# Value copies and both layer normalisations on ScalarE, and the value bias added once per batch

## The chip, the cores and the metric

The kernel runs on one core of a Trainium2 chip. A core has five engines with instruction streams of their own: TensorE (PE, with PEld for its weight loads), VectorE (DVE), ScalarE (ACT), GpSimd (POOL) and SyncE (SP, which issues loads). They meet only through semaphores. The metric is the time in microseconds (us) that the device needs for one execution, as a median of several.

## The reference

The input x is 8 sequences of 2048 rows of 256 numbers. Two blocks follow each other, each with a residual and a layer normalisation without weights:

```python
q, k, v = _heads(x, Wq, bq), _heads(x, Wk, bk), _heads(x, Wv, bv)      # 16 heads of 16
qp = relu(einsum('bhsd,hdf->bhsf', q, rw)) + EPS                       # 64 features a head
kp = relu(einsum('bhsd,hdf->bhsf', k, rw)) + EPS
kv = einsum('bhsf,bhsd->bhfd', kp, v)
out = einsum('bhsf,bhfd->bhsd', qp, kv) / (einsum('bhsf,bhf->bhs', qp, kp.sum(axis=2)) + EPS)
x = layernorm(x + out @ Wo + bo)
# feed-forward: a gated MLP of width 1024 plus a mixture over 1024 experts
mlp = silu(x @ Wg + bg) * (x @ Wu + bu) @ Wd + bd
w = silu(x . down_embed[idx]) * softmax(scores); experts = sum_k w * up_embed[idx]   # top 8 of 1024, 4 heads
x = layernorm(x + mlp + experts)
```

Since v = x Wv + bv, the product kv equals (kp times x Wv) plus bv times the sum of kp over the sequence; the kernel has this sum anyway, as a 33rd column of ones beside the values.

## The kernel before, in words

Rows are handled in 32 groups of 512 (four tiles of 128 rows), four groups to a batch (a sequence). The loop has 35 iterations, numbered 4 to 38. In iteration `it` five stages work on different groups: key work of group it (`kv`: transposes, k, v, key features `kp`, and `sum`, which adds kp times v into `kv_sum`), attention of group it-4 (`at`), routing of group it-5 (`rt`), the feed-forward of group it-6 (`ff`) and the last normalisation and the store of group it-7 (`last`). The first four groups' key work is done in a fill ahead of the loop. Iterations 7 to 31 have all five stages; I call them the full ones. From 32 on there is no key work.

An iteration has 8 steps, c = 0 to 7. Each step does 128 columns of the feed-forward: on TensorE the products gate, up and dots into two PSUM banks in turn (`ring`), then the output products into `y_bank`. ScalarE applies Silu to gate and to dots (`ff_gate`, `ff_dots`), VectorE forms `gate` and `wexp` from them (`ff_h`, `ff_wexp`). Between these stand small pieces of the other stages, which share four PSUM banks (`step_bank`) in a fixed rotation: a piece can start only when the bank's last user has been read. Every engine's order is written out by hand in its own `body`, so nothing is reordered: an instruction that waits holds up all behind it on its engine.

What the change touches:
- `v` (L914): VectorE adds the bias bv to two tiles of values (128x512) on their way from PSUM to `v_sb`, at steps 2 and 5.
- `norm_scale` (L404 to L409): GpSimd turns variances into 1/sqrt by two small instructions, add and power.
- `norm1` (L982): VectorE normalises the attention output `x1`, four instructions of 128x256, at step 7, behind the last `sum`. TensorE's transposes `next` (L517) of x1 wait for it.
- `norm2` (L1074): the same for the output rows `y_sb`, at step 0 behind `wexp`, before `choose(0)`, whose first instruction writes `cand` (L1004). GpSimd's store waits for it.
- routing: VectorE's `scores`, `choose`, `keep` (L1020), `add_head` (L1033, L1036); GpSimd's `spread` (L430) writes `grid`; ScalarE's Exp (L812, `rt_use`) stands between scores and choose. Exp and Silu need different tables, so a table load stands ahead of each.
- `highs` (ScalarE, L768) and `lows` (VectorE, L894): the rounded and the remaining part of q and k, needed by TensorE's feature products and before their bank is free.

The first two of these lines end step 0 on ScalarE with the Exp; the others begin step 1, with the Silu of gate and then the second half of q's highs:

```python
                    if rt and c == 0:
                        rt_use(0)
...
                    if ff:
                        ff_gate(c)
                    if at:
                        for use in AT_EARLY[c]:
                            at_use(*use)
```

## Time and profile before

| | |
|---|---|
| median of 3 executions | 3860.46 us (3854.98 to 3862.65) |
| profiled execution | 3858.18 us, its span 3856.4 us |
| TensorE busy | 3674.8 us (95%) |
| VectorE busy | 3076.9 us (80%) |
| ScalarE busy | 1339.8 us (35%) |
| GpSimd busy | 1675.2 us (43%) |
| mean granted TensorE clock | 0.978 |

The span is the time from the first to the last instruction of the profiled execution. Busy shares are averages: TensorE is busy nearly all the time, VectorE four fifths of it, ScalarE a third. In the timeline, entries of one line that follow each other are merged (x4 is four instructions). A matmul's start is that of its place in TensorE's queue, so a group behind another can begin some tenths of a microsecond before its first column moves.

### The profile page before, as it was taken

The numbers are of one execution on the slowest core, as the hardware profiler recorded it, in microseconds if no ns is written. First come the engines' busy times: TensorE is split into PE (matmuls) and PEld (weight loads), VectorE is DVE, ScalarE is ACT, GpSimd is POOL, SyncE is SP. The second block draws the span as 40 slices with busy tenths as digits, with TensorE's granted clock in tenths as the row PEclk, the third lists the DMA queues.
The fourth block names the chain that finished last, engine by engine and source line by source line (L and its number), as shares of the span: only waits on it lengthen the run. The fifth ranks groups of instructions, "written<-read, shape, count | busy, mean of one in ns | idle before, by whom it ended". The sixth has DMA issues, their size and how long they took to land. (4 is left out here: it accounts for less than half of the span.)

```text
span 3856.4 us, 51959 instructions
## 1 busy us (share of the span) xinstructions
PE 3674.8 (95%) x19388; PEld 3095.6 (80%) x19388; DVE 3076.9 (80%) x5947; ACT 1339.8 (35%) x1990; POOL 1675.2 (43%) x1004
## 2 busy tenths in 40 slices
PE   8969999999999999999999999999999999999988
PEld 7758888888788888888888887888888888777766
DVE  2388888888788878888878888888888888999983
ACT  3323333333333333333333333333333333333321
POOL 0144444444444444454444454444444444555541
PEclk8769999999999999999999999999999999999999
DMA  3000000000000000000000000000000000000000
GB/s 111 17 12 6 12 17 17 17 12 12 12 18 17 17 12 12 15 14 17 17 12 12 17 12 17 17 12 12 17 12 17 17 6 12 12 11 12 6 6 12
DMA packets 23337, 61.15 MB, mean 16 GB/s; under 512 B 5552, under 2 KB 10032, under 8 KB 23088
## 3 DMA queue, kind: packets, MB, share of 16 engines
q1 hardware_dynamic: 18480, 41.04, 3.4%
q0 software_dynamic: 4608, 16.78, 1.1%
q8 instruction: 157, 2.57, 0.3%
q14 instruction: 92, 0.75, 0.1%
HBM read 41.04 MB, written 16.78 MB: 15 GB/s over the span
## 5 line engine op out<-in xcount | busy, mean ns | idle before, releaser
L430 POOL TENSOR_TENSOR grid<-ex 128x1024 f32<-128x1024 f32 x512 | 1245.6, 2440 | 626.3 <-ACT ex L812 286.7
L1020 DVE SCALAR_TENSOR_TENSOR grid<-grid,best 128x1024 f32<-128x1024 f32 x512 | 736.8, 1439 | 31.0 <-POOL grid L430 30.2
L1036 DVE SCALAR_TENSOR_TENSOR prob<-grid,rz,prob 128x1024 f32<-128x1024 f32 x384 | 694.6, 1809 | 3.4
L687 PE MATMUL y_bank<-wd_sb,gate 128*128 128x256 f32 x2048 | 625.2, 387 | 15.6 <-DVE wexp L1058 15.6
L689 PE MATMUL y_bank<-up_sb,wexp 128*128 128x256 f32 x2048 | 612.3, 381 | 0.0
L595 PE MATMUL ring<-x1T_hl,downT_hl 128*128 128x512 f32 x1536 | 417.5, 407 | 19.0 <-ACT gate L817 19.0
L689 PEld LDWEIGHTS y_bank<-up_sb,wexp 128*128 128x128 f32 x2048 | 391.7, 191 | 54.0
L595 PE MATMUL ring<-x1T_hl,wg_hl 128*128 128x512 f32 x1536 | 423.6, 411 | 7.9 <-DVE gate L1052 7.7
L595 PE MATMUL ring<-x1T_hl,wu_hl 128*128 128x512 f32 x1536 | 418.0, 407 | 0.0
L421 POOL TENSOR_SCALAR qp<-qp 128x512 f32<-128x512 f32 x256 | 217.0, 848 | 432.4 <-ACT qp L803 421.0
L687 PEld LDWEIGHTS y_bank<-wd_sb,gate 128*128 128x128 f32 x2048 | 355.9, 192 | 58.3 <-issue 29.9
L595 PEld LDWEIGHTS ring<-x1T_hl,downT_hl 128*128 128x128 f32 x1536 | 277.5, 189 | 85.7 <-ACT gate L817 30.4
L822 ACT ACTIVATE wexp<-ring 128x512 f32<-128x512 f32 x256 | 153.1, 598 | 556.2 <-PE ring L595 555.5
L595 PEld LDWEIGHTS ring<-x1T_hl,wu_hl 128*128 128x128 f32 x1536 | 284.5, 188 | 71.8 <-issue 14.4
L817 ACT ACTIVATE gate<-ring,bg_sb 128x512 f32<-128x512 f32 x256 | 176.4, 689 | 474.2 <-PE ring L595 473.2
L595 PEld LDWEIGHTS ring<-x1T_hl,wg_hl 128*128 128x128 f32 x1536 | 276.0, 189 | 75.4 <-issue 14.9
L783 ACT ACTIVATE kp<-step_bank 128x512 f32<-128x512 f32 x236 | 140.8, 597 | 410.7 <-PE step_bank L559 410.1
L416 POOL TENSOR_TENSOR xb<-xb,bo_sb 128x1024 f32<-128x1024 f32 x32 | 75.2, 2350 | 470.6 <-PE step_bank L517 470.6
L407 POOL TENSOR_SCALAR rstd<-mv 128x4 f32<-128x4 f32 x64 | 15.0, 234 | 570.5 <-DVE mv L945 570.5
L621 PEld LDWEIGHTS step_bank<-kv_blocks,qp 128*128 128x128 f32 x2048 | 252.2, 195 | 8.7 <-DVE ex L996 1.6
L621 PE MATMUL step_bank<-kv_blocks,qp 128*128 128x34 f32 x2048 | 243.5, 275 | 1.3 <-DVE ex L996 1.3
L566 PEld LDWEIGHTS step_bank<-v_sb,kp 128*128 128x128 f32 x1856 | 231.3, 197 | 10.6 <-issue 3.5
(146 smaller groups left out, 5693.2 us busy)
## 6 DMA issues: line engine op xcount, KB each, us to landing
xb<-in_L_attn_x SPq DMA_DIRECT2D x34, 512.0 KB, 3.5
out_y<-x POOLq DMA_DIRECT2D x32, 512.0 KB, 3.1
xa<-in_L_attn_x SPq DMA_DIRECT2D x30, 512.0 KB, 3.4
prob<-in_L_ffn_down_embed SPq DMA_DIRECT2D x1, 1024.0 KB, 5.9
prob<-in_L_ffn_Wg SPq DMA_DIRECT2D x1, 1024.0 KB, 8.7
prob<-in_L_ffn_Wu SPq DMA_DIRECT2D x1, 1024.0 KB, 10.5
wd_sb<-in_L_ffn_Wd SPq DMA_DIRECT2D x1, 1024.0 KB, 11.4
up_sb<-in_L_ffn_up_embed SPq DMA_DIRECT2D x1, 1024.0 KB, 12.0
```

The costliest lines, as they stand in the source:

```text
L421: pool.tensor_scalar(qp[:, j % 4], qp[:, j % 4], ATTN_EPS, 1.0, ALU.add, ALU.mult).then_inc(qp_eps, 1)
L430: pool.tensor_tensor(grid[:, h % 2], bcast(ex[:, h, 0:NX].unsqueeze(2), [P, NX, NK]), bcast(ex[:, RH + h, 0:NK].unsqueeze(1), [P, NX, NK]) ...
L566: mm = pe.matmul(bank[:, c * VW:(c + 1) * VW], lane.kp[:, c * P:(c + 1) * P], lane.v[:, j % 2, c, :], start=(c == 0), stop=(j < T - 1), sk ...
L595: mm = pe.matmul(bank[:], st if swap else wt, wt if swap else st, start=(k == 0 and i == 0), stop=(k == KD - 1 and i == 2))
L621: mm = pe.matmul(at_bank[:, (2 * t + c) * W:(2 * t + c + 1) * W], qp[:, (2 * j + c) % 4, t * P:(t + 1) * P], kv_blocks[:, 2 * j + c].rearr ...
L687: pe.matmul(rows, gate[:, c % 2, t * P:(t + 1) * P], wd_sb[:, c, :], start=(c == 0 and t % 2 == 0), stop=False, skip_group_check=True)
L689: mm = pe.matmul(rows, wexp[:, c % 2, t * P:(t + 1) * P], up_sb[:, c, :], start=False, stop=(c == C - 1), skip_group_check=True)
L783: read_by(act.activation(lane.kp[:, (j % 2) * G:(j % 2 + 1) * G], bank[:], ACT.Relu), "kv", a, kind, j)
L817: act.activation(gate[:, c % 2], ring[c % 2][:], ACT.Silu, bias=bg_sb[:, c:c + 1]).then_inc(ring_act, 1)
L822: act.activation(wexp[:, c % 2], ring[c % 2][:], ACT.Silu).then_inc(ring_act, 1)
L1020: marks["keep", h] = rt_steps.mark(dve.scalar_tensor_tensor(out=g, in0=g, scalar=best[:, h, TOP - 1:TOP], in1=g, op0=ALU.is_ge, op1=ALU.mult))
L1036: ins = dve.scalar_tensor_tensor(out=row, in0=g, scalar=rz[:, h:h + 1], in1=row, op0=ALU.mult, op1=ALU.add, accum_out=mass[:, 0:1] if h == ...
```

## The change

ScalarE copies the values without a bias. Both normalisations become an Identity activation with a scale (rstd) and a bias per row, on ScalarE; GpSimd prepares the bias, minus mean times rstd, with two more small instructions. `norm1` now stands behind `ff_gate(7)` and ahead of the last key features' relu, `norm2` behind the Exp of step 0 and ahead of `ff_gate(1)`. At the end of each batch VectorE adds bv times the summed key features to `kv_sum` before it copies it to `kv_blocks`; clearing `kv_sum` is a memset now.

```diff
@@ GpSimd
                 pool.tensor_scalar(rstd[:], mv[:, :, 1], LN_EPS, None, ALU.add).then_inc(s_own, 1)
-                pool.wait_ge(s_own, g + 1)
-                pool.tensor_tensor(rstd[:], rstd[:], neg_half[:], ALU.pow).then_inc(s_out, 1)
+                pool.tensor_scalar(mv[:, :, 0], mv[:, :, 0], -1.0, 1.0, ALU.mult, ALU.mult).then_inc(s_own, 1)
+                pool.wait_ge(s_own, 3 * g + 1)
+                pool.tensor_tensor(rstd[:], rstd[:], neg_half[:], ALU.pow).then_inc(s_own, 1)
+                pool.wait_ge(s_own, 3 * g + 3)
+                pool.tensor_tensor(mv[:, :, 0], mv[:, :, 0], rstd[:], ALU.mult).then_inc(s_out, 1)
@@ ScalarE
-                if kind in ("v", "sum"):
+                if kind == "sum":
                     return
                 bank = bank_of("kv", a, kind, j)
                 act.wait_ge(*full("kv", a, kind, j))
-                if kind == "turn":
+                if kind == "v":
+                    read_by(act.copy(lane.v[:, :, :, 0:2 * DK],
+                                     bank[:].rearrange("p (t c w) -> p t c w", t=2, c=FC)), "kv", a, kind, j)
+                elif kind == "turn":
...
+                def norm1():
+                    act.wait_ge(rstd1_ready, m + 1)
+                    for t in range(T):
+                        act.activation(x1[:, t, :], x1[:, t, :], ACT.Identity, bias=mv1[:, t, 0:1],
+                                       scale=rstd1[:, t:t + 1]).then_inc(x1_ready, 1)
+
+                def norm2():
+                    act.wait_ge(rstd2_ready, it - LAST_LAG + 1)
+                    for t in range(T):
+                        act.activation(y_sb[:, t, :], y_sb[:, t, :], ACT.Identity, bias=mv2[:, t, 0:1],
+                                       scale=rstd2[:, t:t + 1]).then_inc(y_ready, 1)
+
...
                     if ff:
                         ff_gate(c)
+                    if at and c == C - 1:
+                        norm1()
                     if at:
                         for use in AT_EARLY[c]:
                             at_use(*use)
...
                     if rt and c == 0:
                         rt_use(0)
+                    if last and c == 0:
+                        norm2()
@@ VectorE
-                dve.tensor_scalar(kv_sum[:, :, 0:2 * DK], bv_sb[:].rearrange("p (c w) -> p c w", c=FC),
-                                  ATTN_EPS * S, None, ALU.mult).then_inc(sum_cleared, 1)
+                dve.memset(kv_sum[:, :, 0:2 * DK], 0.0).then_inc(sum_cleared, 1)
...
-                elif kind == "v":
-                    dve.wait_ge(*full("kv", a, kind, j))
-                    read_by(dve.tensor_tensor(lane.v[:, :, :, 0:2 * DK],
-                                              bank[:].rearrange("p (t c w) -> p t c w", t=2, c=FC),
-                                              bcast(bv_sb[:].rearrange("p (c w) -> p c w", c=FC).unsqueeze(1),
-                                                    [P, 2, FC, 2 * DK]), ALU.add), "kv", a, kind, j)
...
-                    if at and c == 7:
-                        norm1()
...
-                    if last and c == 0:
-                        norm2()
...
             def batch_end(b):
 
                 dve.wait_ge(*drained("kv", (b + 1) * BG - 1, "sum", T - 1))
+                bias = cand[:].rearrange("p h a b -> p (h a b)").rearrange("p (c w) -> p c w", c=FC)
+                dve.tensor_tensor(bias, bv_sb[:].rearrange("p (c w) -> p c w", c=FC),
+                                  bcast(kv_sum[:, :, 2 * DK:VW], [P, FC, 2 * DK]), ALU.mult).then_inc(sum_biased, 1)
+                dve.wait_ge(sum_biased, 2 * b + 1)
+                dve.tensor_tensor(kv_sum[:, :, 0:2 * DK], kv_sum[:, :, 0:2 * DK], bias, ALU.add).then_inc(sum_biased, 1)
+                dve.wait_ge(sum_biased, 2 * b + 2)
```

ScalarE from the Exp of step 0 (a table load and the activation that writes `ex`) to the highs of k at step 1 in a full iteration, after the change (line numbers are those of the changed file):

```order
L818 ACT_TABLE_LOAD [waits rt_dve]
L818 ACTIVATE ex<-ex 128x576 [waits bank_read1]
L829 ACTIVATE x<-x,mv,rstd 128x256 [waits rstd2_ready]
L829 ACTIVATE x<-x,mv,rstd 128x256 x3
L835 ACT_TABLE_LOAD [waits y_full]
L835 ACTIVATE gate<-ring,bg_sb 128x512 [waits ring_full]
L771 ACTIVATE qT_hl<-step_bank,bq_sb 64x512 [waits bank_full3]
L771 ACTIVATE qT_hl<-step_bank,bq_sb 64x512
```

Before, the same stretch had no normalisation between the Exp and the table load for Silu:

```order
L812 ACT_TABLE_LOAD [waits rt_dve]
L812 ACTIVATE ex<-ex 128x576 [waits bank_read1]
L817 ACT_TABLE_LOAD [waits y_full]
L817 ACTIVATE gate<-ring,bg_sb 128x512 [waits ring_full]
L768 ACTIVATE qT_hl<-step_bank,bq_sb 64x512 [waits bank_full3]
L768 ACTIVATE qT_hl<-step_bank,bq_sb 64x512
```

The four instructions of `norm2` (they write x, which y_sb shares with x1) now stand ahead of the Silu of gate and of the second half of q's highs. On VectorE the same place before, from the first lows of q to the first add of a head:

```order
L894 SCALAR_TENSOR_TENSOR qT_hl<-step_bank,bq_sb,qT_hl 64x512 [waits q_high] x2
L1077 TENSOR_SCALAR x<-x,mv,rstd 128x256 [waits rstd2_ready]
L1077 TENSOR_SCALAR x<-x,mv,rstd 128x256 x3
L1004 TENSOR_TENSOR cand<-ex 128x256 [waits rt_exp]
L1009 MAX best<-cand 128x8 [waits rt_dve,pool_prep]
L1009 MAX best<-cand 128x8 x3
L1012 TENSOR_REDUCE zsum<-best 128x4 [waits rt_dve]
L1014 RECIPROCAL rz<-zsum 128x4 [waits rt_dve]
L1020 SCALAR_TENSOR_TENSOR grid<-grid,best 128x1024 [waits spread_ready]
L894 SCALAR_TENSOR_TENSOR qT_hl<-step_bank,bq_sb,qT_hl 64x512 [waits q_high] x2
L1033 TENSOR_SCALAR prob<-grid,rz 128x1024 [waits bank_full0,rt_dve]
```

After the change the two L1077 rows are gone and all others stand as they were: VectorE goes from the lows of q straight to `cand`, which waits for the Exp. And VectorE at the start of an iteration that opens a batch, after the change (`x<-y_bank` is the first read of the output rows):

```order
L1056 TENSOR_TENSOR prob<-prob,mass 128x1 [waits rt_dve]
L1140 TENSOR_TENSOR cand<-bv_sb,kv_sum 128x256 [waits bank_read1]
L1143 TENSOR_TENSOR kv_sum<-kv_sum,cand 128x8x32 [waits sum_biased]
L1147 COPY kv_blocks<-kv_sum 64x8x16 [waits sum_biased]
L1148 COPY kv_blocks<-kv_sum 64x8
L1147 COPY kv_blocks<-kv_sum 64x8x16
L1148 COPY kv_blocks<-kv_sum 64x8
L880 MEMSET kv_sum 128x8 [waits blocks_ready]
L881 MEMSET kv_sum 128x8x32
L1078 TENSOR_TENSOR x<-y_bank,bd_sb 128x512 [waits y_stored,bank_full3,y_full]
```

The two L114x instructions are new here, each waited for by the next; the last memset took the place of a 128x256 multiply.

## Rows read from the trace of the kernel before

**Rows 1.** Busy time by stretch, full iterations: length, engines (instructions), TensorE clock, DMA

```profile
420.00:3300.00 2880.00, 2804.98 (x15093) 2373.70 (x15092) 2372.98 (x4641) 1041.22 (x1542) 1294.33 (x775) 1.00 0.04 14
```

**Rows 2.** Waits of PE from 420 to 3300 us: total, times, longest

```profile
PE step_bank L517 <- DVE ex L996: 36.0, 24, 2.2
...
PE step_bank L531 <- DVE kT_hl L894: 35.3, 25, 1.4
```

**Rows 3.** Timeline, one full iteration: start, duration, work [idle before <- releaser]

```profile
2018.13 1.38 DVE L1077 TENSOR_SCALAR x<-x,mv,rstd 128x256 f32<-128x256 f32 x4
...
2018.58 0.69 ACT L812 ACTIVATE ex<-ex 128x576 f32<-128x576 f32 x1
...
2019.43 0.42 DVE L1004 TENSOR_TENSOR cand<-ex 128x256 f32<-128x256 f32 x1
...
2020.58 0.69 ACT L817 ACTIVATE gate<-ring,bg_sb 128x512 f32<-128x512 f32 x1
...
2021.16 1.38 ACT L768 ACTIVATE qT_hl<-step_bank,bq_sb 64x512 fp32r<-64x512 f32 x2
2021.44 1.93 PE L595 MATMUL ring<-x1T_hl,downT_hl 128*128 128x512 f32 x6
...
2022.96 1.51 DVE L894 SCALAR_TENSOR_TENSOR qT_hl<-step_bank,bq_sb,qT_hl 64x512 fp32r<-64x512 f32 x2
...
2024.51 1.01 DVE L1033 TENSOR_SCALAR prob<-grid,rz 128x1024 f32<-128x1024 f32 x1
...
2036.00 1.99 PE L531 MATMUL step_bank<-wv_sb,xaT 128*128 128x256 f32 x8 [1.42 <-DVE kT_hl L894]
```

**Rows 4.** Groups of instructions by line: busy us, mean ns | idle before, releaser

```profile
L783 ACT ACTIVATE kp<-step_bank 128x512 f32<-128x512 f32 x236 | 140.8, 597 | 410.7 <-PE step_bank L559 410.1
...
L963 DVE TENSOR_TENSOR x<-step_bank,den 128x256 f32<-128x256 f32 x128 | 54.3, 424 | 4.4
```

**Rows 5.** Timeline of ScalarE, preparation: a copy of 256 columns

```profile
81.92 0.43 ACT L756 COPY grid<-ring 128x256 f32<-128x256 f32 x1
```

**Rows 6.** Timeline, an iteration without key work, about the same place

```profile
3493.23 1.66 PE L595 MATMUL ring<-x1T_hl,downT_hl 128*128 128x512 f32 x6 [0.99 <-ACT gate L817]
...
3498.05 0.75 DVE L1033 TENSOR_SCALAR prob<-grid,rz 128x1024 f32<-128x1024 f32 x1
```

**Rows 7.** Timeline, end of the full iteration of Rows 3

```profile
2104.35 0.69 ACT L817 ACTIVATE gate<-ring,bg_sb 128x512 f32<-128x512 f32 x1
...
2109.94 1.87 PE L566 MATMUL step_bank<-v_sb,kp 128*128 128x33 f32 x16
```

**Rows 8.** Timeline, start of an iteration that opens a batch

```profile
976.35 1.07 PE L517 MATMUL step_bank<-ident_r,xa 128*128 128x128 f32 x4 [2.21 <-DVE ex L996]
```

**Rows 9.** Timeline of SyncE, residual loads of three successive iterations

```profile
829.34 0.33 SPq L375 DMA_DIRECT2D xb<-in_L_attn_x  x1
...
944.14 0.33 SPq L375 DMA_DIRECT2D xb<-in_L_attn_x  x1
...
1061.59 0.33 SPq L375 DMA_DIRECT2D xb<-in_L_attn_x  x1
```

**Rows 10.** Busy time by stretch, right behind the wait of Rows 8

```profile
978.00:982.00 4.00, 4.00 (x11) 2.23 (x10) 0.82 (x2) 1.65 (x5) 0.00 (x0) 0.77 0.42 131
```

**Rows 11.** Timeline, end of the first iteration

```profile
169.44 1.04 POOL L409 TENSOR_TENSOR rstd<-rstd,neg_half 128x4 f32<-128x4 f32 x1
169.78 2.58 PE L566 MATMUL step_bank<-v_sb,kp 128*128 128x33 f32 x16 [0.79 <-ACT kp L783]
...
176.13 1.94 PE L517 MATMUL step_bank<-ident_r,x 128*128 128x128 f32 x8 [1.90 <-DVE x L985]
```

**Rows 12.** Timeline, end of the second iteration

```profile
257.36 1.94 PE L566 MATMUL step_bank<-v_sb,kp 128*128 128x33 f32 x16 [0.79 <-ACT kp L783]
...
258.39 1.07 POOL L409 TENSOR_TENSOR rstd<-rstd,neg_half 128x4 f32<-128x4 f32 x1
...
274.98 1.94 PE L517 MATMUL step_bank<-ident_r,x 128*128 128x128 f32 x8 [14.28 <-DVE x L985]
```

More of the change, by code:

```diff
@@ L147, in block_kernel @@
         k_high, xs_ready = sem("k_high"), sem("xs_ready")
-        blocks_ready, sum_cleared = sem("blocks_ready"), sem("sum_cleared")
+        blocks_ready, sum_cleared, sum_biased = sem("blocks_ready"), sem("sum_cleared"), sem("sum_biased")
         xa2_loaded = sem("xa2_loaded")
@@ L906, in kv_use @@
                 lane, i = in_lane(a)
-                if kind not in ("k", "v", "sum"):
+                if kind not in ("k", "sum"):
                     return
@@ L980, in norm1_stats @@
                     statistics(x1, stats, mv1, at_steps)
-                def norm1():
-                    dve.wait_ge(rstd1_ready, m + 1)
-                    for t in range(T):
-                        dve.tensor_scalar(x1[:, t, :], x1[:, t, :], mv1[:, t, 0:1], rstd1[:, t:t + 1],
-                                          ALU.subtract, ALU.mult).then_inc(x1_ready, 1)
                 def scores(t):
@@ L1072, in y_rows @@
                     statistics(y_sb, stats, mv2, y_steps)
-                def norm2():
-                    dve.wait_ge(rstd2_ready, f + 1)
-                    for t in range(T):
-                        dve.tensor_scalar(y_sb[:, t, :], y_sb[:, t, :], mv2[:, t, 0:1], rstd2[:, t:t + 1],
-                                          ALU.subtract, ALU.mult).then_inc(y_ready, 1)
                 def uses(kinds):
```

## The prediction

> **What bounds the kernel now.** I read the busy time by stretch first. In the 25 full iterations (420 to 3300 us) TensorE is busy 2805 of 2880 us, so an iteration lasts 115.2 us and TensorE idles 3.0 us of it; VectorE is busy 2373, ScalarE 1041 [rows 1]. Nothing can be won there beyond 75 us, and an engine that makes TensorE wait loses at once. Then the table of waits, for what those 75 us are: 36.0 us at the second transpose of xa at step 0, whose bank `scores(0)` on VectorE must read first, and 35.3 us (25 times, never over 1.4) at the values of step 2, whose bank the second `lows` of k must free [rows 2]. Both name VectorE as the late engine. Last the timeline between them, to see what VectorE hangs on, since taking work off it pays only where it has no other wait.
>
> There the reader sees this. `norm2` runs on VectorE at 2018.13 for 1.38 us, beside the Exp, which ends at 2019.27; `cand` starts at 2019.43, as soon as either allows [rows 3]. ScalarE then switches tables, and the Silu of gate(1) ends at 2021.27. TensorE's dots(1) begins at 2021.44 in the same PSUM bank that this Silu reads, so it has 0.12 us to spare if it starts 0.05 us behind the Silu, as it did in an iteration where it had to wait (the Silu ended at 3493.18, dots at 3493.23 [rows 6]). Then come q's second highs at 2021.16, and VectorE's lows of them at 2022.96. So the tightest place of the iteration is on ScalarE, the engine that is idle two thirds of the time, right where the change puts `norm2`.
>
> **The change, part by part.**
>
> *norm2 in the full iterations.* The trace has no Identity of 128x256 with two per-row operands. A copy of 256 columns took 0.43 us [rows 5]. One per-row bias cost 0.09 (Silu with bias 0.69 [rows 3], Relu without 0.597 [rows 4], both 128x512). Neighbours overlap by 0.11: the Silu starts at 2020.58 and runs 0.69, the highs start at 2021.16 [rows 3]. So one takes 0.43 + 2 x 0.09 = 0.61, and starts 0.50 after the last; four need 0.1 + 4 x 0.50 = 2.1 us. This I take. Bounds: four of 0.43 with that overlap and free operands, 1.4; four of 0.69 without overlap, 2.8. The rule against the change is in the Trainium skill, ScalarE: Activation LUTs, Rules for kernel authors: multiply and add belong on VectorE. The trace agrees as far as it goes, 1.38 us for the four on VectorE [rows 3] against my 2.1. By the same page's figures (What ACT_TABLE_LOAD costs: 186 ns, 0.833 ns a column, 93 ns for each per-row operand, 93 ns of overlap) the four would be 2.07 us, an estimate that would leave the sum as it is.
>
> rstd was there before 2018.13, when VectorE used it [rows 3]; even 1.1 us later it is in time for an Exp that ends at 2019.27. So everything on ScalarE from the Silu of gate(1) on moves by T = 2.1. Two engines feel it.
> TensorE: dots(1) starts at 2021.27 + 2.1 + 0.05 = 2023.42 and not at 2021.44. About 0.3 of the difference is only queue time (a group behind a long one is stamped early: this one shows 1.93 us, one that had waited 1.66 [rows 3, 6]). TensorE is late by 1.7.
> VectorE: the lows could start 0.72 us behind the highs, at 2021.88 + 2.1 = 2023.98, and not at 2022.96: 1.0 late. The scaling that follows took 1.01 beside a GpSimd `spread` [rows 3] and takes 0.75 alone [rows 6]; moved later it runs alone, so 0.26 comes back, and VectorE is 0.75 late. From there to the lows of k it has no idle time in the timeline, so it keeps these 0.75.
> Both meet at the values of step 2 (2036.00, wait 1.42 [rows 3]). TensorE arrives 1.7 late, which its wait takes in but for 0.3; VectorE frees the bank 0.75 late. The later one decides: **0.75 us an iteration**, and 25 x 0.75 = **19 us**. With T between 1.4 and 2.8 this is 0.05 to 1.45 an iteration, 1 to 36 us.
> VectorE's 1.38 us less at step 0 is worth 0.1 at most, since `cand` waits for the Exp.
>
> *norm1 and the values, full iterations: nothing.* The Silu of gate(7) ends at 2105.04, norm1 then runs to 2107.2 and the last relu of kp to 2107.8; the `sum` on TensorE that needs it starts at 2109.94 [rows 7]. What VectorE saves lies ahead of its wait for the x1 transposes, whose place TensorE's full queue sets. If that cover were gone, norm1 would cost up to 2.1 each time. The value copies (some 0.6 us) fall into idle time of ScalarE: it waits 410 us in all for the kp products alone [rows 4]. On VectorE they stood ahead of waits for an Exp or for TensorE.
>
> *Batch starts.* At six of the eight (iterations 8 to 28) VectorE's copies to kv_blocks lie on the way to scores(0), and TensorE's wait is 2.21 [rows 8] where it is 1.25 otherwise (36.0 us in 24 waits, six of them of 2.21, leave 18 of 1.26 [rows 2]): their 0.96 us goes straight into the time. Added are two 128x256 operations like the one of 0.424 us [rows 4], each waited for, 0.95 in all; the memset may save 0.1. 6 x 0.85 = **5 us**, with 3 and 7 as ends.
>
> *The clock.* Two of those six waits of 2.21 us were followed by a lowered clock, 1.2 instead of 2.4 GHz for part of a stretch (mean 0.77 [rows 10]). The iteration around it, from one residual load to the next, took 117.45 us; the one before took 114.80 [rows 9]. Less the 0.96 that is 1.7 us for one fall. The waits become 3.1 us; I count two more falls, **3 us** (0 to 7).
>
> *The first two iterations.* In iteration 4 norm1 stands ahead of the last relu of kp and waits for GpSimd. Its power ends at 170.48; with two more small instructions (0.3 each, a guess between nothing and the power's own 1.04) rstd is there at 171.1, norm1 ends at 173.2, the relu at 173.8, and `sum` starts 4.1 us after its 169.78 [rows 11]. It and what belongs to it took until 174.2; the transposes come at 178.3 and not at 176.13: +2.2. In iteration 5 TensorE waited 14.28 us for norm1, which VectorE reached only behind its routing [rows 12]. On ScalarE it ends at about 262.2, `sum` starts at 262.9, the transposes at 266.5 and not 274.98. Of those 8.5 us VectorE's routing gives back half (the lows of x1 and the clamp still stand behind it, it is earlier by norm1's 1.4 and does not wait again for x1): -4.7. It also drops two value additions in iterations where it is the late engine, -0.9. Together **-3 us** (-7 to +3).
>
> *From iteration 32 on.* VectorE is the late engine in four of them, so TensorE's longer wait at dots(1), 0.99 now [rows 6], 3.1 then, is partly taken in by later waits; I count half a microsecond of it and 0.5 for GpSimd's two extra instructions ahead of spread: 4 x 1.0. In iteration 37 norm2 stands before gate(1) with nothing to hide it: 1.5. Behind the last matmul GpSimd adds 0.7, ScalarE 2.1 - 1.4 = 0.7. Together **7 us** (3 to 14).
>
> The sum is 19 + 5 + 3 - 3 + 7 = 31 us. Against the profiled execution's 3858.18 us (its span and 1.8 around it) this is 3889. The median shown is 2.3 higher, and I predict for the median: 3860.46 + 31 = 3891.5, say **3891 us**.
>
> **The rivals.**
>
> *Hidden after all* (same). ScalarE is idle two thirds of the time; if the four instructions took 1.4 us, VectorE's lows would be on time within 0.1 and TensorE's delay would vanish in its wait. For it only that bound speaks, against it the 0.12 us of slack at dots(1). 0 + 3 + 0 - 5 + 5: 3864.
>
> *Faster: VectorE is relieved where it is late.* Both big waits name VectorE. If norm2 delayed `cand`, its 1.38 would come off both waits' common chain and each full iteration would win up to the 1.4 us wait at step 2: 3860 - 35 + 5 - 7 + 3 = 3826. It decides where `cand` could start earlier than the Exp's end by more than q's highs come later, and `cand` at 2019.43 is 0.16 behind the Exp's end [rows 3]. So only an Exp moved ahead, or T under 1.1 with the larger gain at the start, would lead there.
>
> *Slower: the clock falls in every full iteration.* Two waits of 1.25 and 1.4 us within 23 now leave the clock at full rate [rows 1, 2]; a third of about 1.4 between them, as it would show at dots(1), may not. 25 x 1.7 = 42 more: 3933. For it, that 2.21 us sufficed twice in six; against it, that no single new wait is longer than the 1.4 that never did. The Trainium skill says in TensorE: Matmul & The Clock Gate, The HAM clock gate, that the clock follows how busy the engine was just before; rows 8 and 10 fit that.
>
> **How the numbers follow.** The forecast has 0.70, and its own range is 3872 to 3915 (T from 1.6 to 2.8, the other terms at mixed ends). Hidden 0.10, faster 0.06, clock in every iteration 0.14. The range 3868 to 3926 leaves out the faster case, nearly all of the hidden one, and the clock case but for a fall in some of the iterations only: about 0.2. A measurement tells some 0.2% from no change, 7.7 us. Faster by more: 0.06. Within: 0.09, most of the hidden case. Slower: 0.85.
>
> **What would show it.** Right, if in a full iteration a wait of TensorE at the dots line for ScalarE's Silu appears (some 1.4 us), the wait at the values of step 2 shrinks to about 0.7 and does not vanish, ScalarE's four Identity instructions take about 2.1 us behind the Exp, VectorE now waits for the Exp at `cand` and for q's highs at the lows, and residual loads lie 115.5 us apart instead of 114.8; if batch starts show 3.1 us waits; if the 14.28 us wait falls to under 5. Wrong, if dots(1) starts without a wait, if the distance of loads grows by over 1.5 us, or if the clock falls outside of batch starts.

## The result

The changed kernel takes 3886.95 us (median of 4, 3881.49 to 3888.57) against 3860.99 (4 runs of the kernel before): a ratio of 1.0068 [1.0050, 1.0085]. It is 26 us slower; 31 were forecast. The spans of the two profiled executions differ by 30.4 us (3886.8 against 3856.4).

The page of the kernel after, busy time: VectorE lost 138 us, ScalarE gained 156, GpSimd 12.

```profile
PE 3694.0 (95%) x19388; PEld 3106.0 (80%) x19388; DVE 2939.3 (76%) x5643; ACT 1495.7 (38%) x2310; POOL 1686.8 (43%) x1132
```

Waits of TensorE from 420 to 3300 us, after. Line numbers are those of the changed file; L520 and L534 answer to L517 and L531 of [rows 2], L598 is the line of the matmuls of gate, up, dots and routing.

```profile
PE step_bank L520 <- DVE ex L1005: 42.3, 24, 3.2
PE ring L598 <- ACT gate L835: 28.6, 24, 1.3
PE step_bank L534 <- DVE kT_hl L915: 12.3, 25, 0.5
```

The second row is new. The third has lost two thirds, so most of the new wait is the old one met earlier; the first has grown by 6.3 us, nearly all of it at batch starts. In sum 83.2 us where 71.3 stood.

The timeline of a full iteration after, at the place of [rows 3]:

```profile
2037.49 0.69 ACT L818 ACTIVATE ex<-ex 128x576 f32<-128x576 f32 x1
2038.08 2.06 ACT L829 ACTIVATE x<-x,mv,rstd 128x256 f32<-128x256 f32 x4
2038.21 0.42 DVE L1013 TENSOR_TENSOR cand<-ex 128x256 f32<-128x256 f32 x1 [1.19 <-ACT ex L818]
...
2041.45 0.69 ACT L835 ACTIVATE gate<-ring,bg_sb 128x512 f32<-128x512 f32 x1
2042.04 1.38 ACT L771 ACTIVATE qT_hl<-step_bank,bq_sb 64x512 fp32r<-64x512 f32 x2
2042.19 1.65 PE L598 MATMUL ring<-x1T_hl,downT_hl 128*128 128x512 f32 x6 [1.25 <-ACT gate L835]
2042.74 1.51 DVE L915 SCALAR_TENSOR_TENSOR qT_hl<-step_bank,bq_sb,qT_hl 64x512 fp32r<-64x512 f32 x2 [1.03 <-ACT qT_hl L771]
...
2055.52 2.00 PE L534 MATMUL step_bank<-wv_sb,xaT 128*128 128x256 f32 x8 [0.50 <-DVE kT_hl L915]
```

Read it from the top: norm2's four instructions take 2.06 us behind the Exp, the Silu of gate follows a table load later, and both of its followers now wait, TensorE 1.25 us at dots(1) and VectorE 1.03 us at q's lows. VectorE waits at `cand` too, for an Exp that it used to meet. At the values TensorE still waits, now 0.50 where [rows 3] have 1.42. The wait of 1.25 understates the delay at dots(1): the group now lasts 1.65 us where [rows 3] show 1.93, and the 0.28 between them was time in the queue. So TensorE is 1.53 us late there, gets 0.92 back at the values and keeps 0.61, nearly all of the 0.65 that an iteration loses. The sum of the waits, 11.9 us more in this window, does not show this.

SyncE's residual loads after, around an iteration that opens a batch:

```profile
835.45 0.33 SPq L375 DMA_DIRECT2D xb<-in_L_attn_x  x1
950.91 0.33 SPq L375 DMA_DIRECT2D xb<-in_L_attn_x  x1
1070.08 0.33 SPq L375 DMA_DIRECT2D xb<-in_L_attn_x  x1
```

Their distances measure iterations: 115.46 and 119.17 here, where [rows 9] have 114.80 and 117.45. Below, "ordinary" is the median of the 18 distances between iteration 6's load and the last one that do not open a batch, and "openings" is the sum of the six that do. All kernels of this study in one table (time: median, and that of the kernel before in the same comparison; distances from the profiled execution):

| kernel | time | before | ratio [95%] | ordinary | openings |
|---|---|---|---|---|---|
| before | | | | 114.80 | 698.0 |
| after | 3886.95 | 3860.99 | 1.0068 [1.0050, 1.0085] | 115.45 | 713.5 |
| n2_dve | 3869.28 | 3860.02 | 1.0022 [1.0013, 1.0031] | 114.81 | 706.8 |
| n2_half | 3863.42 | 3860.02 | 1.0002 [0.9994, 1.0011] | 114.67 | 701.7 |
| n2_double | 3928.18 | 3860.02 | 1.0173 [1.0159, 1.0187] | 117.28 | 720.9 |
| n2_late | 3871.31 | 3860.02 | 1.0026 [1.0015, 1.0037] | 114.68 | 701.5 |
| n2_gate | 3885.82 | 3861.09 | 1.0061 [1.0047, 1.0075] | 115.44 | 712.4 |
| v_dve | 3880.56 | 3860.66 | 1.0053 [1.0040, 1.0066] | 115.44 | 702.8 |
| n1_dve | 3887.78 | 3860.66 | 1.0072 [1.0059, 1.0085] | 115.43 | 712.6 |
| n2_only | 3878.42 | 3860.66 | 1.0047 [1.0033, 1.0061] | 115.43 | 703.4 |
| be_late | 3866.93 | 3861.48 | 1.0013 [1.0004, 1.0022] | 115.44 | 693.0 |
| stats_late | 3845.39 | 3861.48 | 0.9956 [0.9943, 0.9970] | 114.17 | 693.1 |
| all_moved | 3788.17 | 3861.48 | 0.9809 [0.9795, 0.9822] | 112.63 | 681.0 |
| before_moved | 3806.77 | 3861.48 | 0.9855 [0.9842, 0.9869] | 113.42 | 682.4 |

For the changed kernel the account of the two profiles is: 18 ordinary iterations +11.9 us, six openings +15.5, everything up to iteration 6's load +0.1, from the last full load to the end +2.9 (722.5 to 725.4). That is the 30.4.

### The profile page after: what moved, and what is told of

Same layout as the page of the kernel before. It is cut to its first block, busy times and chain, and to the rows that moved or that the text cites. A ratio compares the mean times of both kernels' runs of the same rounds, so it can differ in the third digit from the quotient of the medians.

```text
span 3886.8 us, 52103 instructions
## 1 busy us (share of the span) xinstructions
PE 3694.0 (95%) x19388; PEld 3106.0 (80%) x19388; DVE 2939.3 (76%) x5643; ACT 1495.7 (38%) x2310; POOL 1686.8 (43%) x1132
## 4 chain that ended last, share of the span: by engine, by line
PE 65%; DVE 21%; issue 6%; ACT 6%; POOL 1%; SPq 0%; DVEq 0%; DMA 0%; ACTq 0%; POOLq 0%
PE ring L598 16%; PE y_bank L690 9%; PE y_bank L692 9%; PE step_bank L569 5%; PE step_bank L534 5%; DVE prob L1045 5%; PE step_bank L624 5%; DVE grid L1029 4%; PE step_bank L562 3%; PE step_bank L598 2%; PE step_bank L520 2%; PE step_bank L526 2%; PE step_bank L670 2%; PE step_bank L615 2%; DVE gate L1061 1%
## 5 line engine op out<-in xcount | busy, mean ns | idle before, releaser
L1029 DVE SCALAR_TENSOR_TENSOR grid<-grid,best 128x1024 f32<-128x1024 f32 x512 | 765.4, 1495 | 53.4 <-POOL grid L433 52.5
L598 PE MATMUL ring<-x1T_hl,downT_hl 128*128 128x512 f32 x1536 | 415.1, 406 | 52.6 <-ACT gate L835 52.6
L598 PE MATMUL ring<-x1T_hl,wg_hl 128*128 128x512 f32 x1536 | 425.0, 412 | 1.2 <-DVE gate L1061 1.1
L598 PE MATMUL ring<-x1T_hl,wu_hl 128*128 128x512 f32 x1536 | 418.3, 408 | 0.0
L598 PEld LDWEIGHTS ring<-x1T_hl,downT_hl 128*128 128x128 f32 x1536 | 278.5, 191 | 128.4 <-ACT gate L835 77.8
L598 PEld LDWEIGHTS ring<-x1T_hl,wu_hl 128*128 128x128 f32 x1536 | 284.4, 188 | 72.0 <-issue 14.4
L598 PEld LDWEIGHTS ring<-x1T_hl,wg_hl 128*128 128x128 f32 x1536 | 277.7, 190 | 68.0 <-issue 16.4
## 6 DMA issues: line engine op xcount, KB each, us to landing
prob<-in_L_ffn_Wu SPq DMA_DIRECT2D x1, 1024.0 KB, 10.7
```

The lines of the kernel that those rows point to most:

```text
L598: mm = pe.matmul(bank[:], st if swap else wt, wt if swap else st, start=(k == 0 and i == 0), stop=(k == KD - 1 and i == 2))
L1029: marks["keep", h] = rt_steps.mark(dve.scalar_tensor_tensor(out=g, in0=g, scalar=best[:, h, TOP - 1:TOP], in1=g, op0=ALU.is_ge, op1=ALU.mult))
```

## Experiments: where norm2 stands

**n2_dve.** norm2 back on VectorE, nothing else undone.

```diff
@@ ScalarE
-                    if last and c == 0:
-                        norm2()
@@ VectorE, behind uses(AT_LATE[c])
+                    if last and c == 0:
+                        norm2()
```

On VectorE it is `tensor_scalar` with rstd2 and the prepared bias, multiply and add.

> The changed kernel with norm2 alone back on VectorE, at its old place (GpSimd's two extra instructions and everything else of the change stay). Theory (norm2 on ScalarE is late at dots(1) and at the lows, worth 0.64 us a full iteration): ordinary full iterations fall from 115.43 to 114.8 us, and with some 4 us of the last iterations the kernel is 14 to 20 us faster than the changed one, 3867 to 3873 us; the batch starts keep their longer wait (distance about 119). Rival 'GpSimd's longer chain or the value copies cost it': ordinary iterations stay at 115.4, total 3885 or more.

Measured 9.3 us above the kernel before, where the changed kernel is 26 above: norm2 is worth about 17 of them. Ordinary iterations are at 114.81 and the wait at dots(1) is gone. The openings keep most of their length. Waits of TensorE, 420 to 3300 us:

```profile
PE step_bank L520 <- DVE ex L1003: 42.5, 24, 3.2
PE step_bank L534 <- DVE kT_hl L913: 32.8, 25, 1.4
PE ring L598 <- ACT gate L835: 0.8, 1, 0.8
```

**n2_half.** Two of the four tiles on each engine.

```diff
@@ ScalarE, norm2
-                    for t in range(T):
+                    for t in range(2):
@@ VectorE: norm2 for t in range(2, T), at its old place
```

> The changed kernel with two of the four instructions of norm2 on ScalarE and two on VectorE. ScalarE then needs about 1.1 us behind the Exp instead of 2.07. Theory (VectorE's delay at the lows sets the iteration; TensorE's delay goes into its wait at the values): an iteration costs less than 115.43 by about 0.6, since VectorE's lows would move by 1.1 - 1.0 = 0.1: 114.8 to 114.9, total about 3868 to 3874. Rival 'each microsecond on ScalarE costs proportionally': half of 0.64 remains, 115.1, total about 3879.

Ordinary iterations are at 114.67, even a little under those of before: half of the work on ScalarE costs nothing, not half of 0.65. The loss begins only beyond some slack, as the theory said. The time, 3863.42, is below its expected range of 3868 to 3874. In the profiled execution the lowered clock that was expected at batch starts appeared at one of six only; but this execution is the fastest of eleven (3854.08), and how often the clock fell in the one of 3863.42 is not known.

**n2_double.** The same work in eight instructions of 128x128.

```diff
                     for t in range(T):
-                        act.activation(y_sb[:, t, :], y_sb[:, t, :], ACT.Identity, ...).then_inc(y_ready, 1)
+                        for cols in (slice(0, D // 2), slice(D // 2, D)):
+                            ins = act.activation(y_sb[:, t, cols], y_sb[:, t, cols], ACT.Identity, ...)
+                        ins.then_inc(y_ready, 1)
```

> The changed kernel with norm2 on ScalarE in eight instructions of 128x128 in place of four of 128x256, same work, about 3.1 to 3.9 us instead of 2.07 (the fixed part and the two operands eight times). Theory: nothing is left to hide it, so an iteration is longer by the whole of what is added, 1.0 to 1.8 us: 116.5 to 117.2, total 3912 to 3932. Rival 'ScalarE's lateness is absorbed by VectorE's slack at a later wait': under 0.3 us an iteration, total under 3895. Rival 'a longer wait at dots(1) lowers the clock': over 118 in ordinary iterations, with a granted clock under 1 there.

Timeline of an ordinary iteration, and the stretches behind it (length; busy time and instructions of PE, PEld, DVE, ACT, POOL; granted clock; DMA share; GB/s):

```profile
644.97 3.17 ACT L830 ACTIVATE x<-x,mv,rstd 128x128 f32<-128x128 f32 x8
...
650.20 1.90 PE L598 MATMUL ring<-x1T_hl,downT_hl 128*128 128x512 f32 x6 [2.37 <-ACT gate L837]
```

```profile
649.00:652.00 3.00, 1.80 (x7) 1.48 (x8) 1.24 (x2) 2.94 (x5) 1.64 (x1) 0.91 0.03 5
652.00:656.00 4.00, 4.00 (x16) 3.31 (x15) 3.89 (x6) 1.90 (x4) 2.87 (x1) 0.64 0.00 0
656.00:660.00 4.00, 4.00 (x16) 2.75 (x15) 3.94 (x5) 1.36 (x2) 2.64 (x3) 1.00 0.00 0
```

The eight take 3.17 us, 1.11 more than the four. Nearly all ordinary iterations have one of two lengths, 116.6 and 117.3 to 117.5. The shorter is 1.2 above the changed kernel's: beyond the slack each microsecond costs about one. The longer ones are the theory and the rival together: TensorE waits 2.37 us at dots(1), and its clock, 2.4 GHz before, is partly at 1.2 in the 4 us behind (mean 0.64). So the clock rival of the prediction is a real mechanism; at the changed kernel's 1.25 us it did not act, at 2.37 it did, in ten of the 18 ordinary distances.

**n2_late.** norm2 on ScalarE at step 2, where it waits for TensorE anyway.

```diff
@@ ScalarE, behind AT_EARLY[c]
+                    if last and c == 2:
+                        norm2()
@@ GpSimd
-                    if last and c == 1:
+                    if last and c == 2:
                         pool.wait_ge(y_ready, (f + 1) * T)
                         pool.dma_start(out_groups[f], y_sb[:]).then_inc(y_stored, 16)
```

> The changed kernel with norm2 still on ScalarE, but at step 2 behind the first attention use, where ScalarE waits for TensorE anyway; GpSimd's store moves behind it, to step 2. Theory (the place and not the engine costs the 0.64): ordinary iterations return to about 114.8, total 3867 to 3874. Rival 'the engine is the wrong one wherever it stands': ordinary iterations at 115.2 or more, total 3880 or more. The store starts some 18 us later; if the next use of these rows has to wait for it, a wait on y_stored appears on VectorE and the gain is smaller.

Ordinary iterations are at 114.68: it is the place that costs, not the engine. In iterations without key work the steps are shorter, and there the later store is in the way; TensorE's waits from 3300 us on show a wait for the attention rows (which share their buffer with the stored ones), 8.7 us where the changed kernel has 0.9, and VectorE's a wait for the store itself, where the changed kernel has none:

```profile
PE step_bank L670 <- DVE x L978: 8.7, 4, 2.2
DVE den L974 <- DMA out_y<-x: 14.5, 4, 3.6
```

From the last full load to the end it takes 734.0 us instead of 725.4, so the kernel wins 15 us on the changed one where n2_half won 23.

**n2_gate.** Which of the two new waits costs? norm2 behind the Silu of gate(1) and ahead of q's highs: dots(1) is on time, q's lows are not.

```diff
@@ ScalarE
                     if ff:
                         ff_gate(c)
+                    if last and c == 1:
+                        norm2()
...
-                    if last and c == 0:
-                        norm2()
```

> The changed kernel with norm2 on ScalarE behind the Silu of gate(1) instead of ahead of it, still ahead of q's second highs. TensorE's dots(1) then has its old time, VectorE's lows of q are as late as in the changed kernel. Theory (VectorE's lateness at q's lows decides at the values of step 2, and TensorE's wait at dots(1) only uses up idle time that it has there): dots(1) no longer waits, the wait at the values grows from 0.5 back to 1.8 or more, and ordinary iterations stay at 115.3 to 115.5; total 3880 to 3888. Rival 'TensorE's late dots(1) is what costs': ordinary iterations return to 114.8, total about 3870.

```profile
2035.67 2.07 ACT L829 ACTIVATE x<-x,mv,rstd 128x256 f32<-128x256 f32 x4
2035.95 1.93 PE L598 MATMUL ring<-x1T_hl,downT_hl 128*128 128x512 f32 x6
2038.34 1.51 DVE L915 SCALAR_TENSOR_TENSOR qT_hl<-step_bank,bq_sb,qT_hl 64x512 fp32r<-64x512 f32 x2 [1.04 <-ACT qT_hl L771]
...
2051.12 1.99 PE L534 MATMUL step_bank<-wv_sb,xaT 128*128 128x256 f32 x8 [1.53 <-DVE kT_hl L915]
```

dots(1) starts without a wait, and nothing is won: ordinary 115.44, time 3885.82. TensorE waits 1.53 us at the values in place of 1.25 + 0.50. That is less than the 1.8 or more that was expected; some 0.24 us an iteration more are waited for the lows of k at a feature product ahead of the values, 1.77 together (all of 420 to 3300 us):

```profile
PE step_bank L615 <- DVE kT_hl L915: 5.3, 22, 0.3
```

This is the clearest lesson of the case: the new row in the table of waits (28.6 us) was not the loss. VectorE's lateness at q's lows was, and in the changed kernel no row of TensorE's that names VectorE's lows has grown; the one at the values has even shrunk. The reverse, dots(1) late with the lows on time, was not run.

## Experiments: the other parts

**v_dve.** Values' bias per tile on VectorE, and the old end of a batch.

```diff
@@ VectorE
+                elif kind == "v":
+                    read_by(dve.tensor_tensor(lane.v..., bank..., bcast(bv_sb...), ALU.add), "kv", a, kind, j)
@@ batch_end: the two operations on cand and kv_sum go; clearing kv_sum is bv * ATTN_EPS * S again
```

> The changed kernel with the values' bias added per tile on VectorE again and the old end of a batch and clearing (both normalisations stay on ScalarE). Theory (the two extra operations ahead of kv_blocks cost the 3.2 us waits at batch starts, and these lower the clock at five of six): batch-opening iterations fall from about 119 to about 117, the lowered clock appears at two or so of six, total 10 to 14 us under the changed kernel, 3873 to 3877; ordinary iterations stay at 115.4, or rise by up to 0.2 if the value adds on VectorE are in the way. Rival 'the value adds cost VectorE more than the batch end saves': total within 3 us of the changed kernel or above.

The time fell by 6 us (19.9 above before instead of 26), less than the 10 to 14 expected. The openings did lose 10.7 us (713.5 to 702.8; three of the six show the lowered clock, in the changed kernel five), and the ordinary iterations did not move. The rest of the profiled execution is 4.3 us longer, 1.5 up to iteration 6's load and 2.8 behind the last full one. The first lies within what the preparation varies by. Of the second, 1.5 us lie behind a wait of 2.61 us for the last group's `wexp`, which both kernels have: the mean granted clock in the 7 us from there is 0.57 here and 0.79 in the changed kernel. What the rest is stays open.

**n1_dve.** norm1 back on VectorE at the end of step 7.

```diff
@@ ScalarE, behind ff_gate(c)
-                    if at and c == C - 1:
-                        norm1()
@@ VectorE, behind uses(KV_LATE[c])
+                    if at and c == 7:
+                        norm1()
```

> The changed kernel with norm1 alone back on VectorE at the end of step 7. Theory (norm1 is hidden in full iterations on either engine and moves only the first two iterations): ordinary iterations unchanged at 115.4; TensorE's 14 us wait in the second iteration is back and the 4.7 us waits at the sums of the first two are gone; total within 4 us of the changed kernel, 3883 to 3891. Rival 'norm1 on ScalarE delays kp and the sum in each iteration': ordinary iterations shorter by 0.2 or more, total under 3881.

Nothing changed in the full iterations, and the time is within 1 us of the changed kernel's. The second iteration's distance is 113.18 again instead of 110.99; TensorE's wait in it is back at 11.37 us (14.28 before), and those of 4.7 at the sums are 0.8 again.

**n2_only.** The kernel before with norm2 alone on ScalarE (and GpSimd's two extra instructions).

```diff
@@ ScalarE
+                    if last and c == 0:
+                        norm2()
@@ VectorE
-                    if last and c == 0:
-                        norm2()
```

> The kernel before with norm2 alone on ScalarE (values' bias, batch end and norm1 are VectorE's again; GpSimd's two extra instructions are in). Theory: all of 0.64 a full iteration and a few us at the end, none of the batch starts: 3873 to 3880, ordinary iterations 115.4. Rival 'VectorE's value adds and norm2 add up, the loss needs the other parts': ordinary iterations at 114.9 or less, total within 5 us of the kernel before.

17.8 us above before, ordinary 115.43: this one move is the whole loss of the ordinary iterations. With the 6 us of the values and the batch end it makes 24 of the 26.

## Experiments: the waits beside the change

TensorE's largest wait, before and after, is at the second transposes of step 0, behind `scores(0)`. Three moves free it, and then ScalarE.

**be_late.** VectorE's end of a batch goes behind `ff_wexp(0)`.

```diff
                     if ff:
                         ff_wexp(c)
+                    if c == 0 and it <= NG and it % BG == 0:
+                        batch_end(it // BG - 1)
...
-            schedule(dve, body, batch_end)
+            schedule(dve, body, lambda b: None)
```

> The changed kernel with VectorE's end of a batch (bias, copies to kv_blocks, clearing) moved from the start of the iteration to behind wexp(0) of step 0, where VectorE has 1.6 us of idle time. Theory (the batch start costs because these instructions stand ahead of scores(0)): the six waits of 3.2 us fall to 1.25, the clock stays up there, batch-opening iterations fall from about 119 to 115.5 to 116, total about 18 us under the changed kernel, 3868. Rival 'the work only moves and delays q's lows': openings at 117 or more, total above 3878.

```profile
PE ring L598 <- ACT gate L835: 33.2, 25, 3.0
PE step_bank L520 <- DVE ex L1005: 30.9, 24, 1.5
```

Openings are as long as ordinary iterations, 693.0 against 6 x 115.44 = 692.6, and no batch start has the lowered clock: 20 us won for eight instructions moved.

**stats_late.** The statistics of the output rows go behind `scores(0)`.

```diff
@@ VectorE, y_rows
-                    dve.wait_ge(y_read, (f + 1) * 2)
-                    statistics(y_sb, stats, mv2, y_steps)
+                def y_stats():
+                    dve.wait_ge(y_read, (f + 1) * 2)
+                    statistics(y_sb, stats, mv2, y_steps)
...
                     if rt and not odd:
                         scores(t)
+                    if last and c == 0:
+                        y_stats()
```

> The changed kernel with the statistics of the output rows (1.8 us on VectorE) moved behind scores(0); the reads of the output banks stay where they are. Theory (TensorE's 1.25 us wait at the second transposes of step 0 is VectorE's queue ahead of scores(0)): this wait vanishes in every full iteration and falls from 3.2 to about 1.4 at batch starts; ordinary iterations fall from 115.4 to 114.2, with the clock better at some batch starts total 3847 to 3857. Rival 'TensorE meets the same delay at the values or at dots(1) instead': ordinary iterations at 115 or more, total above 3875.

```profile
PE step_bank L534 <- DVE kT_hl L915: 12.6, 25, 0.5
PE step_bank L520 <- DVE ex L1005: 7.8, 6, 1.3
```

The wait at the transposes is left at the six batch starts only, and there 1.3 instead of 3.2. Each ordinary iteration is 1.28 us shorter, the whole of that wait: nothing behind it took it back. The time, 3845.39, is 1.6 us under the expected range.

**all_moved.** Both moves, and Exp and `choose` of step 0 ahead of q's highs and lows. norm2 then stands behind q's first highs.

```diff
@@ ScalarE
-                    if rt and c % 2 == 0 and c:
+                    if rt and c % 2 == 0:
                         rt_use(c // 2)
...
-                    if rt and c == 0:
-                        rt_use(0)
@@ VectorE
-                    if rt and not odd and c:
+                    if rt and not odd:
                         choose(t)
...
-                    if rt and c == 0:
-                        choose(0)
```

> The changed kernel with both moves, and with the Exp of step 0 on ScalarE ahead of the second transposes' copy and q's highs, choose(0) on VectorE ahead of q's lows; norm2 then stands behind q's highs, without a table load in a hurry behind it. Theory (all four engines' waits at the start of an iteration hang on the late Exp and on what stands ahead of scores(0)): the waits of 1.25, 1.25 and 0.5 us all go; ordinary iterations 112.6 to 113.2, batch openings the same, total 3800 to 3820. Rival 'gains end at TensorE's next wait': ordinary iterations at 114 or more, total above 3840.

```profile
1972.75 0.68 ACT L818 ACTIVATE ex<-ex 128x576 f32<-128x576 f32 x1
...
1973.91 1.38 ACT L771 ACTIVATE qT_hl<-step_bank,bq_sb 64x512 fp32r<-64x512 f32 x2
...
1975.31 2.08 ACT L829 ACTIVATE x<-x,mv,rstd 128x256 f32<-128x256 f32 x4
...
1978.70 0.69 ACT L835 ACTIVATE gate<-ring,bg_sb 128x512 f32<-128x512 f32 x1
...
1979.44 1.69 PE L598 MATMUL ring<-x1T_hl,downT_hl 128*128 128x512 f32 x6
...
1992.78 1.99 PE L534 MATMUL step_bank<-wv_sb,xaT 128*128 128x256 f32 x8 [0.47 <-DVE kT_hl L913]
```

3788.17 us, 1.9% under the kernel before; the expectation's range began at 3800. Ordinary iterations came out at 112.63 as expected; openings, which were expected to be the same, are 0.9 longer each. What the expectation had not counted are 8.5 us less than the changed kernel up to iteration 6's load (a few of them the preparation's own spread) and 8.7 less behind the last full one. norm2's 2.08 us and a table load still end in time for dots(1).

**before_moved.** The same three moves in the kernel before; the diff is that of the three above.

> The kernel before with the same three moves (end of batch, statistics, Exp and choose of step 0), so normalisations and value adds are VectorE's. It tells what the change is worth where ScalarE is not pressed. Theory (in full iterations the change then costs and gives nothing, as all is hidden on either engine): ordinary iterations equal to those of all_moved within 0.2, total within 8 us of it. Rival 'VectorE is the bound once the waits are gone': ordinary iterations 0.5 us or more above all_moved, since VectorE carries 3.4 us more.

The theory fell here, and the rival holds. With the moves the change is no longer a loss: it is worth 18.6 us (3806.77 against 3788.17), 0.79 in each ordinary iteration. The timeline of before_moved shows why:

```profile
1987.43 2.97 DVE L1077 TENSOR_SCALAR x<-x,mv,rstd 128x256 f32<-128x256 f32 x4
...
1987.98 1.95 POOL L430 TENSOR_TENSOR grid<-ex 128x1024 f32<-128x1024 f32 x1
...
1991.63 1.51 DVE L892 SCALAR_TENSOR_TENSOR qT_hl<-step_bank,bq_sb,qT_hl 64x512 fp32r<-64x512 f32 x2
...
2004.41 1.99 PE L531 MATMUL step_bank<-wv_sb,xaT 128*128 128x256 f32 x8 [1.31 <-DVE kT_hl L892]
```

On VectorE norm2 now lies beside a `spread` of GpSimd and takes 2.97 us, not the 1.38 of [rows 3]. Three of its four instructions take 0.4 us each; the third takes 1.99, from 1988.09 to just behind the end of the `spread`. So q's lows start 3.6 us behind q's second highs (0.7 in all_moved), and TensorE pays at the values (1.31; all_moved 0.47 at the same place). That this one instruction makes the whole difference is read from the timeline; no run took the `spread` away, and the value adds, which VectorE also carries here, were not tried alone.

## Why the prediction was right, point by point

- *norm2 in the full iterations, 19 us: right in mechanism and nearly in size.* T was forecast at 2.1 and is 2.06. Each iteration lost 0.65 and not 0.75, 16 us over 25: counted from `wexp` of step 0 the lows start 0.88 us later and not 1.0 (1.03 is VectorE's wait for them), and the scaling behind them did fall from 1.01 back to 0.75. The step "both meet at the values, the later one decides, and it is VectorE" is what n2_gate shows. The threshold is shown by n2_half: no cost at two instructions. The wait at dots(1) was forecast at 1.4, is 1.25; that at the values 0.7, is 0.50. The prediction's own terms give 0.47 for the latter (a wait of 1.42, TensorE 1.7 later, the bank 0.75 later); the 0.7 was worked out wrongly, and the sum does not use it.
- *norm1 and the values in full iterations, nothing: right.* n1_dve and v_dve leave ordinary iterations where they were.
- *Batch starts, 5 us: a little small.* The waits grew by 0.99 each and not 0.85 (3.20 forecast as 3.1), 5.9 us in all; the memset gave nothing back (0.27 us for 0.29).
- *The clock, 3 us: too small.* Of the six openings five had a lowered clock, I had counted four; the openings' +15.5 less 6 x 0.65 and 5.9 leaves 5.7 us for three more falls, 1.9 each (forecast 1.7). Together the two terms were 8 and are 11.6. The batch start after, for [rows 8] and [rows 10]:

```profile
984.11 0.76 PE L520 MATMUL step_bank<-ident_r,xa 128*128 128x128 f32 x4 [3.20 <-DVE ex L1005]
```

```profile
986.00:990.00 4.00, 4.00 (x11) 2.16 (x10) 1.06 (x2) 1.74 (x3) 0.00 (x0) 0.76 0.36 121
```

- *The first two iterations, -3 us: right in sign, small, and covered up.* The 14.28 us wait of [rows 12] did go, but in iteration 5 less came of it: the distance fell by 2.25 and not by 4.7, because TensorE then waits 3.89 for the lows of x1, which stay behind VectorE's routing. This is where "half" was too generous; half of the 8.5 is also 4.2 and not the 4.7 that was written, which leaves the sum at -3. The distance before it grew by 0.2, not 2.2. The sum, -2, was taken back by 2.2 us in the preparation, which differs between executions. The two places after:

```profile
265.02 3.60 PE L569 MATMUL step_bank<-v_sb,kp 128*128 128x33 f32 x16 [4.71 <-ACT kp L789]
...
278.85 2.90 PE L598 MATMUL step_bank<-route_hl,x1T_hl 128*128 128x512 f32 x6 [3.89 <-DVE x1T_hl L889]
```

- *From iteration 32 on, 7 us: too large.* It is 2.9 behind the last full load, and some 0.65 of that is iteration 31's, which is a full one. TensorE's waits from iteration 32 on for the Silu of gate grew from 19.0 to 22.8, but those for VectorE's `gate` fell from 7.7 to 1.1. VectorE was the late engine in more places than I gave it, so more of the delay was taken in.
- The errors nearly cancel: 27.4 for full iterations (24 of the 25) where 27 were forecast, 3 elsewhere where 4 were. That the total fits better than several of its terms is luck.
- *The rivals.* "Hidden" failed on T, as its condition said (n2_half is that case with T = 1.1). "Faster by VectorE's relief" needed the Exp moved ahead; all_moved did this and the relief appeared. "Clock falls in every iteration" needed a longer wait, and n2_double shows it at 2.37 us, in about half of the iterations.
- The rule of the Trainium skill that the prediction weighed (ScalarE: Activation LUTs, Rules for kernel authors) holds for the price of the four instructions, 2.06 us against 1.38. It did not decide: in all_moved the dearer place is the faster kernel.

## What to carry to other kernels

An idle share says nothing of a place: look up the few tenths of a microsecond between an engine's next result and who needs it, and put moved work where that engine already waits. When a new wait shows up, test by moving only one of its followers whether it costs anything; the row that grew may be an old wait met earlier. And repair the order first: the same change lost 26 us in one order of the instructions and won 18.6 in another.

## What was not expected of the hardware

- An instruction of VectorE can last as long as the one of GpSimd beside it: the four of norm2 took 1.38 us alone [rows 3] and 2.97 beside `spread`, all of the difference in one that lasted 1.99 and ended just behind the `spread`. The Trainium skill says in SBUF — State Buffer, Who interferes with whom, that VectorE and GpSimd share one pair of ports that one instruction locks whole; these numbers fit that. That the lock is the cause was not tried by itself.
- A wait does not fix what the clock does. With the same 3.2 us at batch starts the clock fell at five of six in the changed kernel, in n1_dve, n2_gate and n2_dve, but at one of six in n2_half and n2_late; after waits of 2.2 us it fell at two of six in the kernel before and at three in v_dve, and at four in n2_only (up to 2.5 us). Each count is of one execution, for n2_half and n2_late the fastest of theirs, and the mean clock of n2_half's eleven runs goes from 0.975 to 0.980 with one code. So chance between executions may be all of it; what decides stays open. After waits of 1.3 or 1.5 us at batch starts (stats_late, be_late) it fell at none.
- The preparation and the first iteration differ in length between executions of code that is the same up to there: the distance between the third residual load and the next is 108.04 us in n2_dve and 100.87 in n2_half, with the granted clock lower in the longer one. Times of one kernel spread by 12 to 14 us (n2_dve 3861.45 to 3873.79, n2_half 3854.08 to 3867.97), more than the smaller effects here; how much of that comes from the start was not counted. The stretch of n2_dve, then of n2_half (TensorE alone: length, busy time, granted clock, DMA share, GB/s):

```profile
120.00:180.00 60.00, 53.82 (x269) 0.76 0.06 18
```

```profile
120.00:180.00 60.00, 52.38 (x280) 0.83 0.06 18
```
